# Score products and value products each issued in two halves of four head pairs

## What is computed

```python
for i in range(6):                                   # the stack, run twice
    x = attn_layer(shift_tokens(x), ...) + x
    x = ffn_layer(shift_tokens(x), ...) + x

def attn_layer(x, Wqkv, qs, ksc, Wo):                # 16 heads of 64, window 32
    q, k, v = split(x @ Wqkv, 3)                     # 128 -> 3 * 1024
    q, k = rotary(l2norm(q) * qs), rotary(l2norm(k) * ksc)
    sim = einsum('bhwie,bhwje->bhwij', bq, bk2) * 8  # 32 queries x 64 keys per window
    attn = softmax(where(mask, -big, sim), -1)
    return einsum('bhwij,bhwje->bhwie', attn, bv2) @ Wo

def ffn_layer(x, g, bln, W1, b1, W2, b2):
    xn = layernorm(x) * g + bln
    a, gate = split(xn @ W1 + b1, 2)                 # hidden size 341
    return a * gelu(gate) @ W2 + b2
```

## Time and profile before

| | us |
|---|---|
| median of 3 runs | 4081.42 |
| lowest and highest of them | 4073.69, 4090.21 |
| the profiled execution, as timed | 4086.48 |
| its span in the trace | 4084.7 |

### The profile page before, as it was taken

How to read it: one execution, slowest core, us unless ns; L and a number is a source line. 1 busy time by engine, 2 the same in 40 slices (tenths; PEclk the granted TensorE clock), 3 DMA queues, 4 the chain that set the end, 5 groups by cost and what they waited for, 6 DMA issues and landing times. The chain is left out here.

```text
span 4084.7 us, 157400 instructions
## 1 busy us (share of the span) xinstructions
PE 3511.6 (86%) x63228; PEld 2234.6 (55%) x63228; DVE 2906.8 (71%) x5185; ACT 2390.6 (59%) x4206; POOL 2086.5 (51%) x2011
## 2 busy tenths in 40 slices
PE   4889898898898888986996689998898898888897
PEld 2556565565565655662221466665565665555564
DVE  3778787787787777873232678887787787787783
ACT  2566665665666656652663456666565565565563
POOL 3556565566565555551001556555556565556551
PEclk7999999999999999997998899999999999999998
DMA  3223223223233222320001322332323322322221
GB/s 95 72 59 97 66 71 88 71 72 85 64 75 91 65 71 69 76 59 3 1 1 32 79 69 70 86 75 77 84 67 80 75 70 78 83 68 69 67 67 37
DMA packets 194569, 273.85 MB, mean 67 GB/s; under 512 B 59788, under 2 KB 85640, under 8 KB 192264
## 3 DMA queue, kind: packets, MB, share of 16 engines
q1 hardware_dynamic: 193800, 263.23, 25.4%
HBM read 35.57 MB, written 1.05 MB: 9 GB/s over the span
## 5 line engine op out<-in xcount | busy, mean ns | idle before, releaser
L1083 POOL TENSOR_TENSOR qkn<-rot,rn 128x512 f32<-128x512 f32 x768 | 784.8, 1043 | 971.6 <-DVE rn L944 971.6
L1077 POOL TENSOR_TENSOR rot<-t 128x512 f32<-128x512 f32 x768 | 977.7, 1273 | 389.2 <-DVE t L923 351.6
L922 DVE TENSOR_TENSOR t<-ps,table 128x512 f32<-128x512 f32 x768 | 528.0, 687 | 297.6 <-ACT sq L733 214.4
L733 ACT ACTIVATE sq<-ps 128x512 f32<-128x512 f32 x768 | 457.4, 596 | 288.0 <-PE ps L508 286.0
L766 ACT ACTIVATE oT<-ps 128x512 f32<-128x512 f32 x384 | 213.6, 596 | 621.6 <-PE ps L582 621.0
L506 PE MATMUL ps<-w_hi,in_hi 128*128 128x512 f16 x1152 | 454.2, 394 | 120.0 <-POOL w_lo L1103 75.6
L923 DVE TENSOR_TENSOR t<-ps,table 128x512 f32<-128x512 f32 x768 | 523.0, 681 | 0.0
L927 DVE TENSOR_REDUCE n<-sq 128x8 f32<-128x512 f32 x768 | 487.5, 677 | 0.0
L970 DVE TENSOR_TENSOR on<-ps,rsum 128x512 f32<-128x512 f32 x384 | 247.5, 687 | 333.7 <-PE ps L572 331.9
L572 PE MATMUL ps<-arena,pT 64*32 64x64 f32 x24576 | 317.7, 228 | 168.5 <-issue 167.7
L507 PE MATMUL ps<-w_lo,in_hi 128*128 128x512 f16 x1152 | 450.9, 391 | 0.0
(11 more groups left out here) (125 smaller groups left out, 5507.1 us busy)
## 6 DMA issues: line engine op xcount, KB each, us to landing
arena<-arena SPq DMA_DIRECT2D x1152, 128.0 KB, 2.4
arena<-arena SPq DMA_DIRECT2D x768, 64.0 KB, 2.0
w_stage<-in_L_ffn_Wqkv SPq DMA_DIRECT2D x12, 1536.0 KB, 6.9
wo_sb<-in_L_ffn_Wo SPq DMA_DIRECT2D x12, 512.0 KB, 5.9
xsh<-xs SPq DMA_DIRECT2D x48, 128.0 KB, 2.7
f_in<-xs SPq DMA_DIRECT2D x48, 128.0 KB, 2.4
xsh<-xs SPq DMA_DIRECT2D x48, 127.8 KB, 2.4
f_in<-xs SPq DMA_DIRECT2D x48, 127.8 KB, 3.1
```

The costliest lines, as they stand in the source:

```text
L733: act.activation(sq[:, c, :], proj[c % 2][:, :], ACT.Square).then_inc(act_sq, 1)
L922: dve.tensor_tensor(t1[:, b, :].rearrange("p (h d) -> p h d", d=DH), src, cos, ALU.mult)
L1077: pool.tensor_tensor(rot[:, c, :], t1[:, c % 2, :], t2[:, c % 2, :], ALU.add).then_inc(pool_add, 1)
L1083: pool.tensor_tensor(qkn[:, 0, c, :].rearrange("p (h d) -> p h d", d=DH), rot[:, c, :].rearrange("p (h d) -> p h d", d=DH), rn[:, c, :].un ...
```

## The change

`scores` and `outputs` get an argument `part`. Part 0 makes the waits and the products of head pairs 0 to 3, part 1 those of head pairs 4 to 7 and the raise of the semaphore. In `step`, part 0 stands where the whole stood. Part 1 of the scores stands behind `project(T, 1)` and the first feed-forward piece; part 1 of the outputs stands behind the second feed-forward piece, directly ahead of `turn_out`. No other engine's list is touched, and no product is added or taken away.

```diff
@@ -530,17 +530,18 @@
                         last = pe.transpose(tr[c % 2][:, i * P:(i + 1) * P], qkn[:, 0, c, i * P:(i + 1) * P], ident[:, :])
                     last.then_inc(pe_tqk, 1)
 
-                def scores(T, s):
+                def scores(T, s, part):
 
                     p = s % 2
-                    pe.wait_ge(dve_on, tile_done(T - 1, 1, 2))
-                    pe.wait_ge(act_k, tile_done(T, 3, 4))
-                    pe.wait_ge(pool_carry, tile_done(T))
-                    for par in range(2):
-                        pe.matmul(sv[par][:, :], identb[:, :],
-                                  maskb[:, 1 if s == 0 else 0, :].unsqueeze(1).broadcast_to([P, HPC, KEYS]),
-                                  start=True, stop=False, skip_group_check=True)
-                    for pair in range(PAIRS):
+                    if part == 0:
+                        pe.wait_ge(dve_on, tile_done(T - 1, 1, 2))
+                        pe.wait_ge(act_k, tile_done(T, 3, 4))
+                        pe.wait_ge(pool_carry, tile_done(T))
+                        for par in range(2):
+                            pe.matmul(sv[par][:, :], identb[:, :],
+                                      maskb[:, 1 if s == 0 else 0, :].unsqueeze(1).broadcast_to([P, HPC, KEYS]),
+                                      start=True, stop=False, skip_group_check=True)
+                    for pair in range(4 * part, 4 * part + 4):
                         for w in range(WPT):
                             for par in range(2):
                                 r = slice(par * DH, (par + 1) * DH)
@@ -548,7 +549,8 @@
                                                  qT[r, p, pair, w * WIN:(w + 1) * WIN],
                                                  kT[r, p, pair, w * WIN:w * WIN + KEYS],
                                                  start=False, stop=True, skip_group_check=True)
-                    last.then_inc(pe_s, 1)
+                    if part == 1:
+                        last.then_inc(pe_s, 1)
 
                 def turn_prob(T, p):
                     pe.wait_ge(act_exp, tile_done(T))
@@ -559,20 +561,22 @@
                                                 prob[:, p, 4 * g + i, :, :].rearrange("q a k -> q (a k)"), ident[:, :])
                         last.then_inc(pe_tp, 1)
 
-                def outputs(T, B, s):
+                def outputs(T, B, s, part):
 
                     v = s % 2
-                    pe.wait_ge(dve_sub, tile_done(T, 1, 2))
-                    pe.wait_ge(act_p, tile_done(T, 1, 2))
-                    wait_apart(pe, v_loaded[s], windows_done(B))
-                    for pair in range(PAIRS):
+                    if part == 0:
+                        pe.wait_ge(dve_sub, tile_done(T, 1, 2))
+                        pe.wait_ge(act_p, tile_done(T, 1, 2))
+                        wait_apart(pe, v_loaded[s], windows_done(B))
+                    for pair in range(4 * part, 4 * part + 4):
                         for w in range(WPT):
                             for par in range(2):
                                 r = slice(par * KEYS, (par + 1) * KEYS)
                                 last = pe.matmul(sv[par][w * WIN:(w + 1) * WIN, pair * DH:(pair + 1) * DH],
                                                  pT[r, pair, w * WIN:(w + 1) * WIN], vw[r, v, w, pair * DH:(pair + 1) * DH],
                                                  start=True, stop=True, skip_group_check=True)
-                    last.then_inc(pe_pv, 1)
+                    if part == 1:
+                        last.then_inc(pe_pv, 1)
 
                 def turn_out(T):
                     pe.wait_ge(dve_on, tile_done(T, 1, 2))
@@ -648,7 +652,7 @@
                     if one:
                         values(T - 1, q_prev if s == 0 else q, (s - 1) % TILES, 1)
                     if two:
-                        scores(T - 2, (s - 2) % TILES)
+                        scores(T - 2, (s - 2) % TILES, 0)
                     if now:
                         if new_layer:
                             pe.wait_ge(pool_wlo, layer_done(L, 1, 6))
@@ -661,6 +665,8 @@
                         f_wo(B - 1, L_prev, 1, 0)
                     if s == 3 and f2:
                         f_w2(B - 2, f1)
+                    if two:
+                        scores(T - 2, (s - 2) % TILES, 1)
                     if now:
                         if new_layer:
                             pe.wait_ge(pool_wlo, layer_done(L, 2, 6))
@@ -678,7 +684,7 @@
                     if s == 3 and f1:
                         f_mean(B - 1)
                     if two:
-                        outputs(T - 2, B if s >= 2 else B - 1, (s - 2) % TILES)
+                        outputs(T - 2, B if s >= 2 else B - 1, (s - 2) % TILES, 0)
                     if s == 0 and f2:
                         f_gate(B - 2, 0)
                     if s == 1 and f2:
@@ -689,6 +695,7 @@
                     if s == 3 and f1:
                         f_var(B - 1)
                     if two:
+                        outputs(T - 2, B if s >= 2 else B - 1, (s - 2) % TILES, 1)
                         turn_out(T - 2)
                     if now:
                         if new_layer:
```

## The result

The change takes 5052.78 us (median of 4 runs, 5044.17 to 5068.32) against 4082.21 us before (4 runs, 4073.69 to 4090.21). The ratio is 1.2404, with a 95% interval of 1.2371 to 1.2438: 24% slower, where 21% had been forecast (4945 us, range 4690 to 5170). Now and then an execution of the kernel before or of a variant runs at a much lower clock (one of the 12 of e6 took 5002.88 us at 0.643), so all times and ratios here are those of the other executions.

What follows compares the result with a forecast made beforehand. TensorE's in-order list was taken as the bound. On 4084.7 us, lost cover added 900, stalls took off 150 and their slow clock 40, new slow clock added 130 and product-size changes 23: 4945 us against the median, range 4690 to 5170.

Steps and rivals of the forecast that it cites:

- The bound: Whole step: TensorE's own list, worked through in order, sets the step length; steps read as 16.6 to 17.1 us.
- First term: From step start to the transposes of the probabilities: lost cover behind the scores adds 2.8 us a step on the mean.
- Second term: From the probabilities' transposes to those of the outputs: lost cover behind the values adds 1.9 us a step on the mean.
- fourth term: TensorE's clock falls after new idle time in three steps of four, 0.9 us each: +130 us, bounds 0 and +307.
- Third term: "Issue" stalls at the small products, read as late instructions: -150 us, bounds 0 and -189; slow clock behind them another -40.
- I take the rest of the step as unchanged: Behind the transposes of the outputs: no added time, VectorE's rotary products following `out_norm` as before and GpSimd gaining time.
- rival of a costlier clock: Two close idle stretches at s = 0 and 3 may drop the clock twice a step: 5,100 to 5,300 us, chance 0.14.
- Fifth term: TensorE changes between full and small products four times more a step, 0.03 us each: +23 us, bounds 0 and +77.
- The sum: Whole kernel: 4084.7 + 900 - 150 - 40 + 130 + 23 = 4947.7 us of span.
- Hidden chains: Gelu, squares and stored values ready earlier in the longer step, so their waits vanish: 4,550 to 4,690 us, chance 0.15.
- Faster: Only the stalls and their slow clock count, if wait before the transposes grows under 1.2 us a step: 3,850 us, chance 0.03.
- The reading that would have shown me wrong: Sign against the forecast: transposes of the probabilities starting within 3 us of the last score product.

Runs made afterwards that it cites:

- e6: Kernel before, value product whole and in place, each half of its head pairs waiting only for its own copy to `pT`: 4059.75 us, ratio 0.9962.
- e4: Kernel before with only the score product in halves, parted by `values(T-1, 1)`, which stood ahead of it; value product whole: 4221.31 us, ratio 1.0354.
- e7: Kernel before with only the value product in halves, parted by `project(T, 3)` from behind the transposes of the outputs; scores whole: 4154.41 us, ratio 1.0198.
- e5: Changed kernel plus useless mask products on TensorE under both bared waits: 4825.19 us, ratio 1.1842 to the kernel before.
- e2: Kernel before with only the value product in halves, as in the change; score product whole in its old place: 4374.42 us, ratio 1.0741.

## Where the prediction held and where it didn't

**The bound** was right: TensorE's list in order. In the change every cause is a wait or slow time on it. The steps of the kernel before had been read too low, though: over all of them the medians are 18.5, 16.9, 17.2 and 18.2 us (s = 0 to 3), not 16.6 to 17.1.

**First term, cover behind the scores.** The steps shown reach the transposes after 9.94 us at s = 2, where 9.8 had been worked out from the earlier trace rows, and after 9.51 at s = 3 (1214.67 to 1224.18) against 9.3. Over 190 steps this stretch grew by 2.7 us on the mean, where 2.8 had been forecast (2.0, 2.8, 3.6 and 3.0 at s = 0 to 3). The wait of 508.3 us is inside the 400 to 550 of the forecast. As it was reasoned, the stored values at s = 2 held their time and weren't drawn forward.

**Second term, cover behind the values.** The 1.48 us bare in each step and the 289.5 us in total were forecast as 1.5 and 290. At s = 3 the stretch from one set of transposes to the other took 8.46 us where 7.5 had been forecast: the transposes at low clock took 0.85 longer and `f_mean` behind them 1.90 us instead of 1.02, which delayed the squares; it is the fourth term at work inside this one.

**Third term, the stalls.** They were taken at -150; "issue" at the small products fell by 226.7 - 48.3 = 178 us. The wait for `pT` had been put at 38 us from one step and was 55.9, so the stalls themselves were 171 and not 189, and all but 1 us of them went. Their cause had been left as a reading, and the trace bears it out. A stalled value product of the kernel before on TensorE, and the instruction queue in the window from 1034 to 1035 us (packets, MB, share):

```profile
1033.07 1.35 PE L572 MATMUL ps<-arena,pT 64*32 64x64 f32 x115 [0.78 <-issue]
1036.51 0.34 PE L572 MATMUL ps<-arena,pT 64*32 64x64 f32 x13 [2.09 <-issue]
```

```profile
q8 instruction: 1, 0.02, 6.8%
```

An instruction packet starts at 1034.21, the first 115 instructions end at 1034.42, and the last 13 start at 1036.51. In the records of that trace all 84 "issue" stalls over 0.9 us at lines 547, 572 and 621 end 2.2 to 3.1 us behind the start of such a packet, with a median of 2.6; of moments taken at random under 15% would. The 76 of e4 and the 76 of e7 end 2.1 to 3.3 us behind one. The reading that fits is that a burst stands when it has used up what is there before the next packet is usable; no run altered the supply itself. It is no rule for every packet: 527 come in, and 84 are followed by such a stall. The change has none of these stalls. So "mostly hidden" (the Trainium skill, Runtime: NRT & Kernel Launch, Instruction fetch mechanics) agrees with this trace by the count of packets, five in six, and not for the bursts that are caught. With nothing to win here the sum would have been 95 us above the span instead of 95 below it: no closer, and wrong in this term.

**Fourth term, the clock.** This is the term that was mis-sized. It was taken at 130 us for new low clock; e5 shows at least 228 (for all low clock that the filler took away). Two things were missed. The forecast counted only the long wait before the transposes of the probabilities, in three steps of four, and not those of the second term, behind which the clock can be low too, as in this step of s = 3 on TensorE, where the transposes of the outputs take 1.97 us instead of 1.09 and the pass behind them 0.63 instead of 0.38:

```profile
1132.29 1.18 PE L575 MATMUL ps<-arena,pT 64*32 64x64 f32 x64
1134.96 1.97 PE L586 MATMUL ps<-ident,on 128*128 128x128 f32 x8 [1.48 <-DVE on L977]
1136.72 0.63 PE L506 MATMUL ps<-w_hi,in_hi 128*128 128x512 f16 x1
```

The same fall refutes the forecast's "I take the rest of the step as unchanged". At s = 3 the stretch from the transposes of the outputs to the next masks went from 5.70 us (median) to 7.88, with 4.4 us of it at the low clock where it had been 2.1 on the mean, and in e5 it was 5.31. Of what e5 gave back, 116 us lay between the two sets of transposes, near the 130 of the forecast, and 88 behind the second set, which the forecast had not counted. The 0.9 us for each fall rested on one late step; at s = 1 and 2 it was 1.15 and 0.95 (50 and 42 us in 44 steps each). The result lies between the forecast and its rival of a costlier clock (5,100 to 5,300), 47 us short of the latter's lower end, and for the reason that the rival gave, two idle stretches close together, but at s = 3 only: at s = 0, which it named too, the filler gave back 28 us in 46 steps.

**Fifth term, the split itself.** It was taken at 23 us with 77 as its bound; e4 shows about 0.25 us a product from start to start, which for two in 192 steps would be 96 us, less what falls under waits. The estimate had looked at one change of product size between masks and scores and not at the small products' own start. The draining at a change of tiling mode (the Trainium skill, TensorEngine Tiling (Array Packing), Key Properties) fits a cost of this kind; no run tells draining from a slower start.

**The sum** was 95 us below the span of 5042.4. The clock explains at least 98 of it; the stalls came out 28 better, the splitting worse by up to about 70, the stretch ahead of the transposes of the probabilities about 20 better. These don't add to a closed account, since low clock inside waits costs nothing, and no run parts them further.

**The rivals.** Hidden chains: refuted by the 192 waits of both kinds, and by the three waits that it let vanish: those for stored values, gelu and squares grew from 64 to 192 us. Faster: its point was 1.2 us of new wait a step, and there are 508.3 + 289.5 - 58.0 - 29.1 = 711 us or 3.7 a step. The reading that would have shown me wrong (transposes within 3 us of the last score) didn't come: it was 3.92.

## What to carry to other kernels

Before a burst is cut in two, ask which half carries the signal, and what runs while the others work on it. The work put between should cover no chain and start none itself, and even then something may have leaned on its place (e4, e7). An in-order engine pays for bared cover twice where its clock falls with idleness: the change stood 798 us before the two sets of transposes, and lost at least 228 to the low clock.

## What the runs showed of the hardware

- In bursts of 128 small products and 128 weight loads in 1.5 us TensorE stood still, inside the burst, for up to 5.7 us. Each of the 84 stalls over 0.9 us ended 2.2 to 3.1 us behind the start of an instruction packet, and 84 of 527 packets had one. With 0.65 us of other work between halves most of the stalls stayed (e4: 37.8 of 59.0 us, e7: 71.0 of 111.8); with a piece of the feed-forward between the halves 5.3 of 111.8 us were left (e2), and in the change, with the new waits as well, about 1 of 170.8.
- A half of 64 instructions takes 0.79 us from its start to that of the next product, the whole 1.42.
- Useless products under a wait made the kernel 228 us faster (4825 against 5053), by holding the granted clock at 0.968 instead of 0.896.
